# The last batch's mixed attention spread over eight PSUM banks, and another interleaving for the wide blocks

## The reference, cut to what matters

```python
xn = x / jnp.maximum(jnp.linalg.norm(x, axis=-1, keepdims=True), 1e-12)
logits = xn @ sn - jax.nn.sigmoid(gates)          # 16 experts
...
w = jax.nn.softmax(masked, axis=-1)               # one weight for each token and expert
def moe_proj(p):
    y = jnp.einsum('nc,ech->neh', x, p)
    return jnp.einsum('ne,neh->nh', w, y)
q, k, v = moe_proj(q_proj), moe_proj(k_proj), moe_proj(v_proj)
scores = q @ k.T / sqrt(h);  attn = softmax(scores);  o = attn @ v
z = jnp.einsum('ne,nh->enh', w, o)
out = jnp.einsum('enh,ehc->nc', z, o_proj)
```

## Time and profile before

| what | value |
|---|---|
| median of the three runs | 2367.44 us |
| the runs | 2361.81, 2367.44, 11244.14 us |
| the profiled execution, its own time | 2362.89 us |
| its span, first to last instruction | 2360.8 us |
| mean granted TensorE clock | 0.952 |
| busy | PE 88%, DVE 84%, PE weight loads 68%, ACT 63%, POOL 41% |

### The profile page before, as it was taken

One profiled execution on the slowest core, in us unless ns is written; L12 is line 12 of the kernel. 1 busy time (PEld: TensorE's weight loads), 2 busy tenths in 40 slices (PEclk: granted clock), 3 DMA queues, 4 the chain that ended last, 5 costly groups with the idle time before them and its releaser, 6 DMA issues. The chain is left out here.

```text
span 2360.8 us, 41642 instructions
## 1 busy us (share of the span) xinstructions
PE 2068.2 (88%) x12569; PEld 1614.0 (68%) x12569; DVE 1973.1 (84%) x7820; ACT 1476.0 (63%) x3639; POOL 959.0 (41%) x1382
## 2 busy tenths in 40 slices
PE   5878788989989899989999899998999899797767
PEld 3556567657966688656876578765886578666545
DVE  1299897989989798998989898897989899896971
ACT  3546467666767666776666666676667767476431
POOL 3233214543354424554164434544255432433432
PEclk9979899999999999999999999999999999899877
DMA  4000101010100101001100101001100001001000
GB/s 184 1 8 1 34 24 32 1 34 1 55 4 1 34 19 39 1 1 35 55 3 1 34 6 52 1 1 34 32 26 1 6 23 55 30 4 52 1 3 3
DMA packets 29503, 55.03 MB, mean 23 GB/s; under 512 B 2914, under 2 KB 10082, under 8 KB 28642
## 3 DMA queue, kind: packets, MB, share of 16 engines
q1 hardware_dynamic: 29282, 52.37, 6.8%
HBM read 51.31 MB, written 1.05 MB: 22 GB/s over the span
## 5 line engine op out<-in xcount | busy, mean ns | idle before, releaser
L232 DVE MATCH_REPLACE8 top_work<-top_eight,top_work 128x256 f32<-128x256 f32 x1664 | 668.4, 409 | 0.0
L234 DVE MAX8 top_eight<-top_work 128x8 f32<-128x256 f32 x1664 | 618.0, 413 | 0.2
L268 POOL TENSOR_TENSOR top_p<-top_p,top_rest 128x512 f32<-128x512 f32 x192 | 244.4, 1273 | 161.4 <-ACT top_rest L261 161.4
L789 PE MATMUL bank<-workP 128*128 128x256 f32 x1024 | 275.5, 393 | 12.4 <-ACT att_pP L927 10.2
L927 ACT ACTIVATE att_pP<-bank,att_tinyP 128x256 f32<-128x256 f32 x512 | 216.0, 480 | 57.1 <-DVE att_tinyP L976 55.3
L789 PEld LDWEIGHTS bank<-workP 128*128 128x128 f32 x1024 | 179.4, 192 | 62.2 <-issue 30.7
L976 DVE TENSOR_REDUCE att_tinyP<-bank 128x2 f32<-128x512 f32 x256 | 173.7, 682 | 25.5 <-PE bank L789 23.5
L234 DVE MAX8 top_lead<-bank 128x8 f32<-128x256 f32 x384 | 145.1, 420 | 42.1 <-PE bank L594 17.8
L261 ACT ACTIVATE top_rest<-top_work,top_nmax 128x256 f32<-128x256 f32 x384 | 173.3, 503 | 11.2 <-DVE top_work L232 10.9
L240 POOL TENSOR_SCALAR top_nmax<-top_lead 128x2 f32<-128x2 f32 x192 | 37.1, 193 | 346.4 <-DVE top_lead L234 345.9
L949 POOL TENSOR_SCALAR workP<-workP,const 128x256 f32<-128x256 f32 x256 | 121.7, 482 | 128.3 <-PE bank L789 106.2
(11 more groups left out here) (335 smaller groups left out, 4646.3 us busy)
## 6 DMA issues: line engine op xcount, KB each, us to landing
gelu_w<-in_pack3w SPq DMA_DIRECT2D x72, 256.0 KB, 3.0
top_qk<-in_pack3w SPq DMA_DIRECT2D x72, 256.0 KB, 2.8
pack<-in_pack SPq DMA_DIRECT2D x1, 4352.0 KB, 19.8
pack<-in_pack SPq DMA_DIRECT2D x1, 2266.0 KB, 9.9
pack<-in_pack SPq DMA_DIRECT2D x1, 1028.0 KB, 7.5
mix_wb<-in_ctx SPq DMA_DIRECT2D x1, 1024.0 KB, 4.9
x_in<-in_x SPq DMA_DIRECT2D x8, 128.0 KB, 2.2
ctx_tok<-in_ctx SPq DMA_DIRECT2D x8, 128.0 KB, 2.4
```

The source lines that it names most:

```text
L232: ins = nc.vector.match_replace(self.work[:, u % 2, j, :], eight, src, GONE)
L234: ins = nc.vector.max(eight, src)
L268: self.k.nc.gpsimd.tensor_tensor(v, v, self.rest[:, :, :], ALU.subtract).then_inc(self.p_ready, 1)
L789: mm = self.k.nc.tensor.matmul(self.banks[u % 2][:, j * T:(j + 1) * T], self.q1[:, u % self.RING, j * P:(j + 1) * P], self.kT, start=True, ...
```

## The change

`ORDER_WIDE` and `ORDER_WIDE_2` become other strings of the same letters (same counts of each). The parameter `alone` goes away. For the last batch alone, `Chunk4` takes a new class, `MixedAttentionInManyBanks`. Its steps 0 to 5 are the old ones. Then: all 16 weight products go out in a row into eight banks (pairs 6, 7, 4, 5 first, which ACT copies; pairs 0 to 3 stay in their banks and are read from there); DVE makes `zT` of pairs 0 to 5 and POOL of pairs 6 and 7; the v products go to bank 4, half of them ahead of the scores and half behind, while DVE and ACT work on the scores in bank 5; the transposes go to bank 6; at the end DVE multiplies six pairs and POOL two. Other blocks' code of `MixedAttention` is as it was.

```diff
 ORDER_WIDE_2 = (
-    "QPPQQQQQQQQPPPPPQPPQQQPQPPPPPPPPPQQPPQPQPPQPQPPPPQQQPPPQPPQQPQPPQQQQQQPPQPQQPQQQQPQPQQQPPQQQQPQPQQQPPQQQQPQQPQ"
+    "QQQPQQQPQQQPQPPPPQPQQPPQQPPPPPPPPPQQPPQQPPQPQPQQQPPPQQQPPPPPPQPQQQQQPPQPPQPQPQQQPQQPQQQPQQPQPQQPQQQPPQQQPQQPQQ"
...
 ORDER_WIDE = (
-    "PPMMPPMMQMQQPQMQPPPMPMMMQMPMPMPQQMMPMMMMMMPMQMPMMQQMPMMQQQPPQQMQPMQQPQQQPMQPMQQPQMPQQMPQQMQMPMMQQQQQQPPMQPQPQQ"
+    "PMMQQMPMPQPMPQQQQMMPPQPQPMMMMPMPMPQMQPMQPMMMMMQMPMMMMMMPMQQPQMPQQQQMPMPQQQQMPQQMPQQQPMPQQQMPMQQQPMMMQQQQPPQPPQ"
...
@@ Chunk4 @@
-        self.mix = MixedAttention(k, "M", k.x[i % 3], i, k.psum[7], 7, i == NB - 1)
+        kind = MixedAttentionInManyBanks if i == NB - 1 else MixedAttention
+        self.mix = kind(k, "M", k.x[i % 3], i, k.psum[7], 7)
...
+class MixedAttentionInManyBanks(MixedAttention):
+    HELD, COPIED, LATER = (0, 1, 2, 3), (6, 7, 4, 5), (6, 7)
+        self.home = [*self.k.psum[0:7], self.bank]
+        self.v_bank, self.s_bank, self.t_bank = self.k.psum[4:7]
...
+    def weights_of(self, i):
+        if i in self.HELD:
+            return self.home[i][:, :].rearrange("p (e t) -> p e t", e=2)
+        return self.wb[:, 2 * i:2 * i + 2, :]
...
+    def pe(self, pe, s):
...
+        if s == 6:
+            pe.wait_ge(self.wT_ready, 1)
+            for i in (*self.COPIED, *self.HELD):
+                for e in (2 * i, 2 * i + 1):
+                    mm = nc.tensor.matmul(self.home[i][:, (e % 2) * T:(e % 2 + 1) * T],
+                                          self.k.part_rows16[:, e:e + 1].broadcast_to([P, P]), self.wT[:, :],
+                                          start=True, stop=True)
+                mm.then_inc(self.wb_ps, 1)
+        if s == 7:
+            pe.wait_ge(self.wb_ready, 2)
+            for i in range(self.PAIRS):
...
+                    nc.tensor.matmul(b[:, 0:T], w["qp"][:, e * D:(e + 1) * D], self.zT[:, e, :], start=(e == 0), stop=False)
+                    mm = nc.tensor.matmul(b[:, T:2 * T], w["kp"][:, e * D:(e + 1) * D], self.zT[:, e, :], start=False, stop=(e == E16 - 1))
+            mm.then_inc(self.qkv_ps, 1)
+            pe.wait_ge(self.wb_ready, 4)
+            self.pe_values(pe, range(self.PAIRS // 2))
+        if s == 8:
+            pe.wait_ge(self.qkv_copied, 2)
+            for j in range(NT):
+                mm = nc.tensor.matmul(self.s_bank[:, j * T:(j + 1) * T], self.qT[:, j * P:(j + 1) * P], self.kT, start=True, stop=True)
+            mm.then_inc(self.scores, 1)
+        if s == 9:
+            self.pe_values(pe, range(self.PAIRS // 2, self.PAIRS)).then_inc(self.qkv_ps, 1)
+        if s == 10:
+            for j in range(NT):
+                pe.wait_ge(self.p_ready, j + 1)
...
+    def dve(self, dve, s):
...
+        if s == 6:
+            for i in range(self.PAIRS - len(self.LATER)):
+                if i in self.HELD:
+                    dve.wait_ge(self.wb_ps, len(self.COPIED) + i + 1)
+                else:
+                    dve.wait_ge(self.wb_ready, self.COPIED.index(i) + 1)
+                self.times(v, i, self.ln.yT[:, :]).then_inc(self.z_ready, 1)
...
+        if s == 12:
+            dve.wait_ge(self.o_copied, 1)
+            for i in range(self.PAIRS - len(self.LATER)):
+                self.times(v, i, self.oT).then_inc(self.zo_ready, 1)
```

More of the change, by code:

```diff
@@ L53 @@
 ORDER_WIDE_2 = (
-    "QPPQQQQQQQQPPPPPQPPQQQPQPPPPPPPPPQQPPQPQPPQPQPPPPQQQPPPQPPQQPQPPQQQQQQPPQPQQPQQQQPQPQQQPPQQQQPQPQQQPPQQQQPQQPQ"
-    "QPQQPQQPPQQQQQQPPQQQPPQPQQPQPPQPPPPQPQQQQQQPPQQPQPPPPPPPPPQPPQQPQQQQQQPPPQQQPPQQQQQPPQQQQQPQQQQQQQQQPPPQQQQPPP"
-    "QQQQQPQQQQQPPPPPPPPQQQQQPPP")
+    "QQQPQQQPQQQPQPPPPQPQQPPQQPPPPPPPPPQQPPQQPPQPQPQQQPPPQQQPPPPPPQPQQQQQPPQPPQPQPQQQPQQPQQQPQQPQPQQPQQQPPQQQPQQPQQ"
+    "QQPPQQQPPQQQPPPQQQQQPPPPQQQQPPPPPQPQQQPPQPQPPPPPPPPQPPPPPQQQPPQQQQQQPQQQQQQQQQPQQPQQQPQPPPQQQQQQQQQQQQQQPPPQQQ"
+    "QQPPPQQQQQPPPQQPPPPPQQQQPQP")
 ORDER_HEADS = (
@@ L61 @@
 ORDER_WIDE = (
-    "PPMMPPMMQMQQPQMQPPPMPMMMQMPMPMPQQMMPMMMMMMPMQMPMMQQMPMMQQQPPQQMQPMQQPQQQPMQPMQQPQMPQQMPQQMQMPMMQQQQQQPPMQPQPQQ"
-    "QQQQQMQQQQPPQQPMPMPPQMMMPQQQQQMQQQQPMPQQQQMQPPMMPPMPPPQPPPMPPQMQQQQMQQPQQQQPPPMQMQQQQQQMMQPPQMQQQPPPQQQQQMMQQQ"
-    "QPPPQQQPPQQQQQPQQQQQQQQQQMMPMQMQQQPQQQQPQPQQMMQMQMPPPMQQPPPQQQPQQP")
+    "PMMQQMPMPQPMPQQQQMMPPQPQPMMMMPMPMPQMQPMQPMMMMMQMPMMMMMMPMQQPQMPQQQQMPMPQQQQMPQQMPQQQPMPQQQMPMQQQPMMMQQQQPPQPPQ"
+    "QQQPMMQQPQQMQPPQQMMPPQQQQMPQQQQMQQQPPQQMQQQPQPQPQMPPMMMMMQPQQPPPMMMPPPQQQQPQQMQPPQQPPQQQQQMPPPQQQQQQMPQQQQQQQQ"
+    "QQPPPMMQQQQQPPQQQPMMMMQQQPQQQQQQMQPQQQQPPQQQQQQMMMPPQQMPPPPQQQQPQP")
 ORDER_HEADS_2 = (
@@ L1853, with __init__ @@
     SUM = 6
-    def __init__(self, k, side, x, batch, bank, gate, alone):
+    def __init__(self, k, side, x, batch, bank, gate):
         self.name = "mixed"
-        self.k, self.x, self.batch, self.bank, self.gate, self.alone = k, x, batch, bank, gate, alone
+        self.k, self.x, self.batch, self.bank, self.gate = k, x, batch, bank, gate
         self.ln = LayerNorm(k, side, "m", x, bank)
@@ L1958, in pe @@
         if 0 <= i < self.PAIRS:
[L1959 to L1962, removed]
+            pe.wait_ge(self.zo2_ready, i + 1)
             for e in (2 * i, 2 * i + 1):
@@ L2037, in pool @@
         i = self.close(s) - self.SUM
-        if 0 <= i < self.PAIRS and (i % 2 == 1 or not self.alone):
+        if 0 <= i < self.PAIRS:
             pool.wait_ge(self.o_copied, 1)
@@ L2111, in dve @@
         i = c - self.SUM
-        if 0 <= i < self.PAIRS and i % 2 == 0 and self.alone:
-            dve.wait_ge(self.o_copied, 1)
-            self.attended(v, i).then_inc(self.zo_ready, 1)
         if i == self.PAIRS + 1:
```

99 lines of the change are left out of this document (added).

## The result

The kernel after took 2334.15 us (median of 4 runs, 2332.08 to 2338.39); the kernel before beside it 2367.99, where one of its four runs took 11244.14 us and is no part of the ratio. The ratio is 0.9871, 95% interval 0.9853 to 0.9890: a gain of 26 to 35 us. By 2% that counts as the same. The forecast was 2344.6, the range 2332 to 2360. The time lies in the range but at its lower end, at the 2335 of rival C.

What follows compares the result with a forecast made beforehand. PE was taken to bound the wide blocks, DVE close behind; the last block was one chain. From 2362.89 us, 15.3 off for the last block, 3 for ORDER_WIDE_2 and 0 for ORDER_WIDE gave 2344.6, range 2332 to 2360.

Steps and rivals of the forecast that it cites:

- rival C: Strings gain: 1.2 us wait gone in all six wide blocks, 5 us from ORDER_WIDE_2; 2335 us, chance 0.12.
- 1, spreading the weights: Last block: 16 weight products issued in a row let the q and k products start 7.0 us earlier.
- 2, q and k: Last block: clock rises 3.8 us after PE turns continuous, weight products counted; q and k products save 1.7 us.
- 3, from there to the last products: Last block, from q and k's end to the last products: 12.2 us instead of 17.5, saving 5.3.
- The cover: Last block: second half of the v products, 3.7 us, hides the 2.6 us from row maximum to scaling.
- 4, the last products: End of the last block: 8.2 us instead of 9.56, with 0.8 allowed for a clock fall; saves 1.3.
- 5, ORDER_WIDE: Six wide blocks: gains and costs cancel, 0 in all, bounds -2 to +3 us a block.
- rival A: Wide blocks: lane P's later start (2.5 us) and POOL's pacing cost 3.5 us each; 2370 us, chance 0.12.
- 6, ORDER_WIDE_2: The one ORDER_WIDE_2 block: lane P's PE work starts about 3 us sooner; 3 us gained, bounds -6 to +2.
- signs named: Last block about 60 us, wide blocks within 2 of 135, ORDER_WIDE_2 block near 139, no PE wait for scaling, held pairs 0.7.
- B: Last block: clock rises late and is at half level for later products, costing 4 us; 2349 us, chance 0.08 in full.
- D: Last block: DVE slow beside POOL even when reading a bank, last products wait 3 us; 2348 us, chance 0.04.

Runs made afterwards that it cites:

- e4: The kernel after, unchanged, measured again: 2339.30 us against 2363.90 for the kernel before, ratio 0.9899.
- e1: The kernel after with both old order strings, so only the last block's new class: 2349.37 us, ratio 0.9934 to the kernel before.
- e5: The kernel after with all 64 value products ahead of the scores instead of half behind them: ratio 0.9904 to the kernel before, last block 65.6 us.
- e6: The kernel after with all eight weight pairs copied to SBUF by ScalarE, none held in its bank: ratio 0.9886 to the kernel before, last block 60.5 us.
- e8: The kernel after plus thrown-away PE products ahead of the gate's transposes (512 columns) and between steps at the last block's start: ratio 0.9859 to the kernel before.
- e3: The kernel before with the new ORDER_WIDE_2 string alone: 2364.62 us against 2363.90, ratio 1.0001.
- e7: The kernel after plus seven thrown-away PE products of 512 columns ahead of the gate's transposes in the last block: ratio 0.9877 to the kernel before.
- e10: The kernel after plus seven thrown-away PE products of 256 columns ahead of the gate's transposes in the last block: ratio 0.9880 to the kernel before.

## Why the prediction came out as it did

*1, spreading the weights.* Forecast 7.0 us earlier, measured 6.8 (q and k start 22.45 us after the block's start, before it was 29.26). Right, terms too: 16 products in 3.59, the held pairs at 0.68.

*2, q and k.* Forecast 14.3 with the clock rising 3.8 us after PE became continuous, the weight products counted. Measured 13.8, with the rise at 3.4. That the weight products count is shown. The delay is no fixed number, though: from the first weight product to the rise it was 3.4 in the kernel after and in e4, 5.0 to 5.5 in e1, e5 and e6, and each us of it cost q and k half a us. So the 3.8 that I took from one trace came out near by luck.

*3, from there to the last products.* Forecast 12.2, measured 11.5. The cover holds as I had it, and e5 shows that it was needed. The transposes took half of my 0.9.

*4, the last products.* Forecast 8.2, with 0.8 for a fall of the clock; measured 7.4, no fall. e8 shows the fall all the same, at 1.6; it is the one of eight such traces that does. The reserve was fair; in this execution it was not drawn. The prediction's sum for the last block, 15.3, came out at 17.1, just over my bound of 17.

*5, ORDER_WIDE.* This is the step that missed, though inside its bounds of -2 to +3 a block. I wrote "I take 0 in all": 1.2 gained at the transposes, against it 0.8 for the later start of lane P and 0.4 for the four steps that POOL paces. The gain was as I had it and more: besides the 1.2, most of a 0.9 us wait 10.6 us into the block goes. I had put the 1.2 down to the two letters Q alone, and not seen that 0.9 of it was DVE's scaling held up beside POOL. Neither of the costs showed. The heads' layer norm on DVE ends 6.6 us after the start in place of 4.0, the 2.5 of rival A. Their sixteen reductions (L976) then lie between 0.7 ahead of the old string's and 1.3 behind, and their last DVE step (L983) starts 4.5 ahead: lane P has slack between its steps, and PE, which bounds the block, had other lanes' work meanwhile. In the list of PE's waits there is none for POOL's products ahead of the last ones. So it is 1.7 a block at equal clock, 7.1 us in the traces and 8 to 15 in the times. What I did wrong was to charge a lane's delay to the block without asking whether that lane's work is what the bounding engine was short of; the view that answers it, PE's waits of a whole block, was before me, and I had used one line of it.

*6, ORDER_WIDE_2.* Forecast 3 gained, measured none (e3). The wait of 5.9 is 4.1 now, as foreseen, but the block's other lane waits more. DVE's waits in this block of e3:

```profile
DVE top_lead L234 <- PE bank L1085: 4.3, 1, 4.3
DVE x L1830 <- POOL moe_accP L1477: 4.1, 1, 4.1
DVE wide_rden L1150 <- PE bank L1107: 2.4, 3, 1.1
DVE rt_nmaxP L1305 <- PE bank L1280: 1.7, 1, 1.7
```

The kernel before has 5.9, 3.4 and 2.1 for the first three of these lines' pairs (L1830, L234 and L1150) and no wait at L1305. At the same 17 us at the half level the block is 141.4 with the new string (e5, e7, e10) against 142.5 with the old, so 1.1 is gained where the clock is alike, and that is below what the times can tell.

*The total.* In the profiled executions 24.5 us went where the sum said 18.3. Part of the fit is luck: the 3 us of ORDER_WIDE_2 that did not come made up for some of the 7.5 of ORDER_WIDE that I had at nothing. And the measured time itself moves between measurements: 2334.15 is 10.5 under the forecast, e4, the same kernel measured again, 5.3. Of the signs named, the wide blocks lie from 132.7 to 134.8, in two cases just outside "within 2 us of 135", and the ORDER_WIDE_2 block is at 142.7 and not near 139; the others came.

*The rivals.* C (0.12) had the size and the half of the mechanism that is in the wide blocks; its other half, 5 us from ORDER_WIDE_2, didn't come, and the last block gave 1.8 more than it said. A, B and D did not come. e5 and e6 show what B and D would have cost: 3.9 us behind an uncovered chain, and 1.6 at the last products with all pairs in SBUF.

## What to carry to other kernels

When an order of steps is rewritten, add up the waits of the engine that bounds the block, before, and ask of each whether the new order fills it; a lane that only started later cost nothing here, where that engine had other work. Compare blocks only at like granted clock: here the same block differs by 2 us from that alone, more than the edit under test. In a chain at the end of a kernel, keeping PE continuous can be worth twice: it hides the other engines' steps, and it keeps the clock, which in e5 was the larger part (3.9 against 2.6 us). And look at what a string puts side by side: if a DVE instruction that PE waits for is longer than its like elsewhere, see which POOL instruction it started behind.

## What was not expected of the hardware

Three short DVE instructions a wide block took as long as a POOL product beside them. The smallest, L1357 on 128 by 16, took 1.27 to 1.28 us in each of the six blocks, started 0.02 to 0.03 us behind L268, and 0.175 us in the ORDER_WIDE_2 block.

The time from PE's first continuous work to the full clock varied from 3.4 to 5.5 us between kernels whose code up to there is the same, and over the same idle pieces of 0.8 and 1.2 us the clock fell in e8 and held in seven other traces. Thrown-away products raise it as well as useful ones (weights at 1.92 us in place of 3.59).

The records of DVE's top-eight instructions were longer in some profiled executions and cost no time. In the wide blocks the mean of MAX8 is 411 ns in the kernel before, 428 to 433 in the kernel after and in e4, and 409 to 413 in e5 to e8 with the same strings; in the block before the last it is 508 and 511, and 404 to 411 in e5 to e8. It isn't the string: e1 and e3, with the old ORDER_WIDE and on e4's chip, have 426 and 423 in a wide block and 466 and 506 in the one before the last. The wide blocks of the new string with 3.4 us at the half level are 133.4 to 133.7 in both kinds, and from the start of one MAX8 to the next instruction it is 0.33 us in both. So a longer record of an instruction isn't yet a slower engine; the distance from one start to the next decides. Why the records differ stays open.
